# Head, expert stages and their joints rebuilt: routing by token, norms on ScalarE, a new order of weight pieces

## What is computed

```python
x = x + ssm(layernorm(x))          # diagonal complex state space, 64 states, then W_out and b_out
x = x + experts(layernorm(x))      # 8 experts, each token takes its 2 best by router logits
x = x + attention(layernorm(x))    # 16 heads of 64, softmax(q k^T + relative bias) v, Wo
x = x + experts(layernorm(x))      # the same expert weights again

# experts(x): g = sigmoid(two largest logits), divided by their sum
for e in range(8):
    ge = sum(g where the token's choice is e)
    out += ge[:, None] * ((silu(x @ w_gate[e]) * (x @ w_up[e])) @ w_down[e])
```

## Time and profile before

| | us |
|---|---|
| median of 3 runs | 902.26 (902.04 to 903.08) |
| profiled execution | 905.03 |
| its span | 903.2 |
| head, to the first expert product | 0 to 74.31 |
| first pass of expert stage 0 (eight steps) | 74.31 to 129.21 |
| other steps of stage 0 | 129.21 to 229.97 |
| between them and the first scores | 229.97 to 244.87 |
| attention's slots | 244.87 to 723.27 |
| its end and the first pass of stage 1 | 723.27 to 791.29 |

### The profile page before, as it was taken

How to read it: one execution, slowest core, us unless ns; L and a number is a source line. 1 busy time by engine, 2 the same in 40 slices (tenths; PEclk the granted TensorE clock), 3 DMA queues, 4 the chain that set the end, 5 groups by cost and what they waited for, 6 DMA issues and landing times.

```text
span 903.2 us, 13948 instructions
## 1 busy us (share of the span) xinstructions
PE 819.9 (91%) x4320; PEld 547.8 (61%) x4320; DVE 658.6 (73%) x1664; ACT 515.1 (57%) x1121; POOL 442.9 (49%) x464
## 2 busy tenths in 40 slices
PE   1867699999779999999999999999999996899997
PEld 0555478888545556556556565565565564688875
DVE  7998477787788776767776767767777646687876
ACT  2214365665466766666566665657656644556664
POOL 3350389998234333433333333334333423789994
PEclk9698899999999999999999999999999997999999
DMA  7001345438300000000000000000000012436621
GB/s 210 3 1 30 85 74 85 90 84 241 122 1 1 1 1 1 1 1 1 1 1 1 1 2 1 1 1 1 1 1 1 1 37 72 96 80 84 79 70 47
DMA packets 53265, 36.40 MB, mean 40 GB/s; under 512 B 2209, under 2 KB 50721, under 8 KB 53201
## 3 DMA queue, kind: packets, MB, share of 16 engines
q1 hardware_dynamic: 53200, 35.61, 17.7%
HBM read 34.35 MB, written 1.25 MB: 39 GB/s over the span
## 4 chain that ended last, share of the span: by engine, by line
PE 75%; DVE 11%; issue 4%; POOL 3%; DMA 3%; ACT 2%; SPq 0%; POOLq 0%; DVEq 0%; ACTq 0%
PE bank L839 13%; PE bank L822 12%; PE bank L809 11%; PE bank L222 10%; PE bank L411 9%; PE bank L224 8%; PE bank L223 8%; PE bank L775 3%; POOL hid_lo L688 3%; DMA gates<-gatesT 1%; DVE x_norm L263 1%; DMA gate_all<-gates 1%; DVE ln_stats L237 1%; DVE prob L884 1%; PE bank L277 1%
## 5 line engine op out<-in xcount | busy, mean ns | idle before, releaser
L1028 POOL TENSOR_SCALAR prob<-prob,inv_total 128x512 f32<-128x512 f32 x256 | 175.1, 697 | 317.3 <-DVE inv_total L873 317.3
L688 POOL TENSOR_TENSOR hid_lo<-hid,hid_hi 128x512 fp32r<-128x512 f32 x128 | 192.1, 1518 | 92.3 <-ACT hid_hi L476 90.4
L977 ACT ACTIVATE prob<-prob,peak 128x512 f32<-128x512 f32 x256 | 185.8, 726 | 47.5 <-DVE peak L884 47.5
L884 DVE CUSTOM_DVE_ANT_0 prob<-bank,bias_band 128x512 f32<-128x512 f32 x256 | 166.6, 689 | 31.0 <-PE bank L809 25.1
L822 PE MATMUL bank<-ident,prob 128*128 128x128 f32 x1024 | 136.5, 277 | 3.1 <-ACT probT L983 1.8
L839 PE MATMUL bank<-probT,v 128*64 128x512 f32 x512 | 138.2, 620 | 0.8 <-ACT oT L988 0.8
L559 DVE TENSOR_TENSOR hid<-hid,gate_all 128x512 f32<-128x512 f32 x128 | 123.6, 970 | 19.0 <-DMA gate_all<-gates 15.2
L822 PEld LDWEIGHTS bank<-ident,prob 128*128 128x128 f32 x1024 | 119.8, 143 | 23.9 <-issue 7.2
L550 DVE TENSOR_TENSOR hid<-silu,bank 128x512 f32<-128x512 f32 x128 | 87.0, 684 | 57.8 <-PE bank L224 39.7
L476 ACT CAST hid_hi<-hid 128x512 fp32r<-128x512 f32 x128 | 78.8, 618 | 61.2 <-DVE hid L559 58.1
L466 ACT ACTIVATE silu<-bank 128x512 f32<-128x512 f32 x128 | 76.1, 599 | 61.8 <-PE bank L224 57.5
(11 more groups left out here) (171 smaller groups left out, 1266.1 us busy)
## 6 DMA issues: line engine op xcount, KB each, us to landing
gate_all<-gates SPq DMA_DIRECT2D x12, 1024.0 KB, 15.5
bias_band<-bias_rows SPq DMA_DIRECT2D x16, 448.0 KB, 11.5
gate_all<-gates SPq DMA_DIRECT2D x16, 256.0 KB, 4.9
w_raw<-in_w_gate SPq DMA_DIRECT2D x16, 128.0 KB, 14.5
w_raw<-in_w_up SPq DMA_DIRECT2D x16, 128.0 KB, 10.5
w_raw<-in_w_down SPq DMA_DIRECT2D x16, 128.0 KB, 8.7
x_res<-in_x SPq DMA_DIRECT2D x4, 256.0 KB, 4.7
out<-x_res SPq DMA_DIRECT2D x4, 256.0 KB, 2.3
```

Source lines behind the costliest of these rows:

```text
L688: nc.gpsimd.tensor_tensor(hid_lo[:, buf, m, :], hid[:, buf, m, :], hid_hi[:, buf, m, :].bitcast(F32), ALU.subtract).then_inc(q["hl"], 1)
L884: nc.vector.tensor_tensor_reduce(out=prob[:, buf, h, :], in0=bank[2 * (n % 2) + h][:, :], in1=row_bias, scale=-1.0, scalar=NEG_START, op0= ...
L977: nc.scalar.activation(prob[:, buf, h, :], prob[:, buf, h, :], ACT.Exp, bias=peak[:, buf, h:h + 1], scale=-1.0, accum_out=total[:, buf, h: ...
L1028: nc.gpsimd.tensor_scalar(prob[:, buf, h, :], prob[:, buf, h, :], inv[:, buf, h:h + 1], 1.0, ALU.mult, ALU.mult).then_inc(a_n, 1)
```

## The change

- **Head.** The state layer's products are plain float32, one where there were three. The angle operations, seven and not eight, come before the norm of rows. The root has 11 links. Where the norm is applied by ScalarE (ln_apply: layer 0, the first expert stage, chunk 0 of attention's, chunk 3 of the second expert stage's), VectorE makes a shift for it. Other copies go to ScalarE. Weights of experts 0 and 1 are split in the head, and for stage 1 in attention's last batch.
- **Routing** is token-wise: 128 tokens are the stationary operand, the router's 16 columns (hi and lo of 8 experts) move, and VectorE adds hi and lo (route_sum). It goes in parts, chunks 0, 1 and 2, 3 in stage 0; chunks 0 to 2 within attention's slots and chunk 3 after them in stage 1. The gates of expert 0 are spread by TensorE into PSUM (route_spread; all chunks in stage 0, chunk 3 in stage 1), the others by DMAs of 256 KB.
- **Order.** First and last pass go by chunk (BY_CHUNK: both experts on chunks 0 and 1, then both on 2 and 3), the middle ones by expert. All are written out. hid has four buffers in the first pass.
- **Weight pieces** are placed by tables: position in the pass, then (par, passes ahead, piece). Two semaphores, `wu` after the up piece and `wd` after the down piece, take the place of `w`.
- **Ends.** The sums of chunks 0 and 1 are turned within the last steps, and in stage 0 the norm statistics of chunk 0 are made there. The last downs and attention's first projections are interleaved, and so are attention's end and the first steps of stage 1.

```diff
+            ln_link(dve, k, nc.vector.tensor_scalar(rstd[:, tiles].bitcast(U32), var[:, tiles].bitcast(U32), -0.5,
                                                     RSQRT_START, ALU.mult, ALU.add))
...
+        def ln_shift(dve, k, c0, c1):
+
+            tiles = slice(c0 * QT, c1 * QT)
+            nc.vector.scalar_tensor_tensor(out=shift[:, tiles], in0=mv[:, tiles, 0], scalar=-1.0, in1=rstd[:, tiles],
+                                           op0=ALU.mult, op1=ALU.mult).then_inc(LN[k]["rs"], 1)
...
+        def ln_apply(act, k, c, group):
+
+            act.wait_ge(LN[k]["rs"], group + 1)
+            for n in range(c * QT, (c + 1) * QT):
+                last = nc.scalar.activation(xn[:, n, :], x[:, n, :], ACT.Identity, bias=shift[:, n:n + 1],
+                                            scale=rstd[:, n:n + 1])
+            last.then_inc(LN[k]["xn"], 1)
...
-        MOE_LAG = 2
+        LAG = 2
+        BY_CHUNK = [(0, 0), (0, 1), (1, 0), (1, 1), (0, 2), (0, 3), (1, 2), (1, 3)]
+        BY_EXPERT = [(0, 0), (0, 1), (0, 2), (0, 3), (1, 0), (1, 1), (1, 2), (1, 3)]
+        ENDS = (BY_CHUNK, BY_CHUNK)
+        INTO_MIDDLE = (BY_EXPERT, BY_CHUNK)
+        MIDDLE = (BY_EXPERT, BY_EXPERT)
+        INTO_LAST = (BY_CHUNK, BY_EXPERT)
...
+        ROUTED = [[(0, 2), (2, 4)], [(0, 3), (3, 4)]]
+        TURN_BANK = [[5, 7], [7, 7]]
+        IN_PSUM = [(0, 1, 2, 3), (3,)]
...
+        FIRST_PIECES = {6: [(0, 1, 0)], 7: [(0, 1, 1)]}
+        MIDDLE_PIECES = {0: [(0, 0, 2)], 1: [(1, 0, 0)], 2: [(1, 0, 1)], 3: [(1, 0, 2)], 6: [(0, 1, 0)],
+                         7: [(0, 1, 1)]}
+        LAST_PIECES = {0: [(0, 0, 2), (1, 0, 0)], 1: [(1, 0, 1)], 2: [(1, 0, 2)]}
+
+        def first_of(order, pos):
+            return order[pos][0] not in [par for par, _ in order[:pos]]
+
...
+            for j in range(QT):
+                tok = slice((c * QT + j) * P, (c * QT + j + 1) * P)
+                dst, both = bank[home][:, j * 2 * E:(j + 1) * 2 * E], rw[:, :, :].rearrange("p r e -> p (r e)")
+                nc.tensor.matmul(dst, xh[:, tok], both, start=True, stop=False)
+                last = nc.tensor.matmul(dst, xl[:, tok], both, start=False, stop=True)
...
+        def route_spread(pe, k, c):
...
+            for j in range(QT):
+                n = c * QT + j
+                last = nc.tensor.transpose(bank[4 + c][:, j * P:(j + 1) * P],
+                                           MEM[k]["gates"][:, n, 0:1].to_broadcast([P, P]), ident[:, :])
+            last.then_inc(q["gb"], 1)
...
+        def gate_up(pe, k, i, order, pos, half, first=False):
+
+            q, m = MOE[k], MEM[k]
+            s, (par_, c) = 8 * i + pos, order[pos]
+            tok = slice(c * BANK, (c + 1) * BANK)
+            if half == 0 and first_of(order, pos):
+                pe.wait_ge(q["wu"], 2 * i + par_ + 1)
...
+        def experts_tensor(pe, k, rest):
+
+            for i in range(1, HALF - 1):
+                for pos in range(8):
+                    expert_step(pe, k, i, INTO_MIDDLE if i == 1 else MIDDLE, pos)
+            for pos in range(8):
+                gate_up(pe, k, HALF - 1, BY_CHUNK, pos, 0)
+                down(pe, k, HALF - 1, INTO_LAST, pos)
+                if pos == 7:
+                    sums_turn(pe, k, 1)
+                gate_up(pe, k, HALF - 1, BY_CHUNK, pos, 1)
+                if pos == 5:
+                    sums_turn(pe, k, 0)
+            rest(lambda: down(pe, k, HALF, ENDS, 0), lambda: down(pe, k, HALF, ENDS, 1))
...
+            lo, hi = PIECES[piece]
+            act.wait_ge(q["ld0"] if par_ == 0 else q["ld1"], 48 * (i + ahead) + 48)
+            if not first:
+                if piece == 2:
+                    act.wait_ge(q["d"], 8 * (i + ahead) - (2 if par_ == 0 else 0))
+                elif par_ == 0:
...
+        def pool_step(pool, k, i, pos, pieces, deep=2, first=False):
+            s = 8 * i + pos
+            low_of(pool, k, s, pos, 0, deep, first and pos < 2)
+            for par_, ahead, piece in pieces.get(pos, ()):
+                weight_low(pool, k, 2 * (i + ahead) + par_, par_, piece)
+            low_of(pool, k, s, pos, 1, deep, first and pos < 2)
+
...
+            def routing(n):
+                if n == MAX_AT:
+                    route_max(dve, 1, 0)
+                if INDEX_AT <= n < INDEX_AT + 2:
+                    c0, c1 = ((0, 1), (1, 3))[n - INDEX_AT]
+                    route_index(dve, 1, 0, c0, c1)
+                if n == WEIGH_AT:
+                    route_weights(dve, 1, 0)
+                if n == PICK_AT:
+                    route_pick(dve, 1, 0)
...
-                pe.wait_ge(LN[0]["lo"], b + 1)
+                pe.wait_ge(LN[0]["hi"], b + 1)
                 if b >= 2:
                     pe.wait_ge(m_z, 4 * (b - 1))
                 for r in range(2):
-                    last = three(pe, bank[2 * (b % 2) + r][:, :], bTh[:, r, :], bTl[:, r, :], xh[:, tok], xl[:, tok])
+                    last = nc.tensor.matmul(bank[2 * (b % 2) + r][:, :], bT[:, r, :], xf[:, tok],
+                                            start=True, stop=True)
...
+            step = lambda pos: expert_step(pe, 0, 0, ENDS, pos, True)
+            both = lambda pos: [gate_up(pe, 0, 0, BY_CHUNK, pos, half, True) for half in range(2)]
+            ln_turn(pe, 1, 0, 4)
+            ln_turn(pe, 1, 1, 5)
+            route_logits(pe, 0, 0, 4)
+            both(0)
+            route_logits(pe, 0, 1, 5)
+            both(1)
+            ln_turn(pe, 1, 2, 6)
+            ln_turn(pe, 1, 3, 7)
+            both(2)
+            route_spread(pe, 0, 0)
+            route_turn(pe, 0, 0)
+            both(3)
+            route_logits(pe, 0, 2, 6)
+            route_logits(pe, 0, 3, 7)
+            route_spread(pe, 0, 1)
+            gate_up(pe, 0, 0, BY_CHUNK, 4, 0, True)
+            down(pe, 0, 0, ENDS, 2, True)
+            gate_up(pe, 0, 0, BY_CHUNK, 4, 1, True)
+            gate_up(pe, 0, 0, BY_CHUNK, 5, 0, True)
+            down(pe, 0, 0, ENDS, 3, True)
+            gate_up(pe, 0, 0, BY_CHUNK, 5, 1, True)
+            route_spread(pe, 0, 2)
+            route_turn(pe, 0, 1)
+            route_spread(pe, 0, 3)
+            down(pe, 0, 0, ENDS, 4, True)
+            gate_up(pe, 0, 0, BY_CHUNK, 6, 0, True)
+            down(pe, 0, 0, ENDS, 5, True)
+            gate_up(pe, 0, 0, BY_CHUNK, 6, 1, True)
+            gate_up(pe, 0, 0, BY_CHUNK, 7, 0, True)
+            down(pe, 0, 0, ENDS, 6, True)
+            down(pe, 0, 0, ENDS, 7, True)
+            gate_up(pe, 0, 0, BY_CHUNK, 7, 1, True)
...
+            experts_tensor(pe, 0, enter)
+            steady()
+            leave()
+            experts_tensor(pe, 1, finish)
...
+            ln_apply(act, 0, 0, 0)
...
-            link(nc.vector.tensor_scalar(ang, ang, 2 * math.pi, PI_BELOW, ALU.mult, ALU.min))
-            nc.vector.tensor_scalar(ang, ang, -PI_BELOW, None, ALU.max).then_inc(s_rot, 1)
...
+            nc.vector.tensor_scalar(ang, ang, HALF_TURN, -HALF_TURN, ALU.min, ALU.max).then_inc(s_rot, 1)
+            for pair in range(2):
+                for c in (2 * pair, 2 * pair + 1):
+                    dve.wait_ge(x_in[c], 16)
+                ln_rows(dve, 0, 2 * pair, 2 * pair + 2)
...
```

More of the change, by code:

```diff
@@ L371, in route, with route_pick @@
+        def route_pick(dve, k, part):
+            m, (c0, c1) = MEM[k], ROUTED[k][part]
+            tiles, sl = (c1 - c0) * QT, slice(c0 * QT, c1 * QT)
+            pick = [m["pick"][:, r, sl] for r in range(2)]
             iota_all = iota8[:, :].unsqueeze(1).to_broadcast([P, tiles, E])
             for r in range(2):
[L373 removed]
+                last = nc.vector.tensor_tensor(pick[r], iota_all, m["topf"][:, sl, r:r + 1].to_broadcast([P, tiles, E]),
@@ new lines, in product, with products @@
+        def product(dve, k, s, pos, half, deep=2, first=False):
+            q, m = MOE[k], MEM[k]
+            dve.wait_ge(q["sg"], 2 * s + half + 1)
+            dve.wait_ge(q["u"], 2 * s + half + 1)
+            if not first:
+                dve.wait_ge(q["hl"], 2 * s + half + 1 - 2 * deep)
+            nc.vector.tensor_tensor(m["hid"][:, pos % deep, half, :], m["silu"][:, half, :], bank[2 * half + 1][:, :],
+                                    ALU.mult).then_inc(q["mul"], 1)
+        def products(dve, k, s, pos, deep=2, first=False):
+            for half in range(MT):
+                product(dve, k, s, pos, half, deep, first)
```

1351 lines of the change are left out of this document (742 added, 609 removed).

## The result

| | before | changed |
|---|---|---|
| median of 4 runs | 902.67 us | 931.28 us (930.04 to 934.97) |
| ratio | | 1.032 (95% interval 1.029 to 1.036) |
| profiled execution, its span | 905.03, 903.2 | 934.97, 933.2 |

What follows compares the result with a forecast made beforehand. TensorE was taken to bound the kernel, busy 91% of the span and nearly full in steady expert steps. Terms -15.8 - 1.4 + 13.8 + 1.4 + 4.2 - 3.0 + 13.8 = +13.0 gave 915.3 us, range 886 to 926.

Steps and rivals of the forecast that it cites:

- a: Head: first states at about 22.9, first expert product at 58.5; -15.8 us (bounds -9 and -20).
- b: First pass of stage 0, now by chunk: old gate waits go, new waits come; -1.4 us (bounds -8 and +4).
- c: Later expert passes: TensorE pauses for w_lo at three places per stage, low clock behind; +13.8 us in each stage.
- d: From the last down group into attention's first scores: sums, turns and norm roots moved; +1.4 us.
- e: Attention: routing of three chunks in its last batch's slots, 3.2 us on TensorE and 1.0 for VectorE; +4.2 us.
- f: Out of attention and through the first pass of stage 1: 65 us against 68.02; -3.0 us (bounds -10 and +3).
- rival 2: Ragged ends come near TensorE's own work and attention absorbs its routing, pauses stay: 898 us; chance 0.20.
- Rival 1: No pauses in the expert passes, since w_lo comes before it is wanted: 887.7 us; chance 0.08.
- Rival 3: Head gains under 9 us and low clock covers more of first passes and pauses: 925 us; chance 0.14.

Runs made afterwards that it cites:

- e4_pool: e2_all, with GpSimd's w_lo of expert 1 and second qk_lo in the head held until after VectorE's norm ahead of the experts: 889.25 us, repeated 890.27.
- e1_middle: Changed kernel with the next pair's up piece made at position 6 instead of 7 in first and middle passes: 903.66 us, ratio to before 0.997.
- e2_all: e1_middle, with the second expert's up piece in the last pass made at position 0 (down piece at 1): 892.10 us, ratio 0.985.
- e3_late: Kernel before, with the next expert's three weight pieces made at chunks 1, 2 and 3 instead of 0, 1 and 2: 975.38 us, ratio 1.078.
- e6_route: e4_pool, with VectorE's routing of chunk 3 at the begin of stage 1 ahead of step 4's products: 880.80 us, repeated 884.18.

## Why the prediction was wrong, step by step

In spans (the profiled execution's forecast of 918.0 less the 1.8 around its span), forecast 916.2, measured 933.2: 17.0 us missing. The mechanism of the largest term, the pauses, was right. The steps that failed are sizes: the low clock behind pauses (3.6 us stood for it in each stage, 7.1 and 6.5 came, and 3.9 more than forecast in the first pass), and the head, where VectorE's norm beside GpSimd was taken at its undisturbed length (10.0 us, 13.7 came). Attention came out 6.0 us under its forecast and hid part of this; without it 23.0 us would be missing. By stretch, change against before:

| stretch | forecast | measured | in e4_pool |
|---|---|---|---|
| a, head | -15.8 | -9.9 | -15.2 |
| b, first pass, stage 0 | -1.4 | +2.9 | -1.3 |
| c and d, to the first scores | +15.2 | +20.6 | +1.9 |
| e, attention | +4.2 | -1.8 | +1.5 |
| f, first pass, stage 1 | -3.0 | -0.1 | -3.9 |
| c, rest of stage 1 and tail | +13.8 | +18.3 | +1.9 |

**c, the mechanism: right.** The waits were forecast at 3.2, 3.2 and 3.8 us in each stage; they are 3.36, 3.36, 3.59 and 3.36, 3.36, 3.60. e1_middle and e2_all take them away, e3_late puts them into the kernel before. The idle VectorE did make the last w_lo quick (0.72), but the two hid_lo ahead of it stood beside VectorE's gate products (L624) and took 3.51 us together, so the pause was not 2.8. Of what part c worked out from the Trainium skill, the quick last piece is so in this trace and the shorter pause is not.

**c, the clock: mis-sized, the first of the failing steps.** I took "two in three of such stretches, 1.2 each" and counted three pauses in each stage. The stretch from the ninth step on also holds the low clock behind the pause at its own start, so there are four, and each costs 1.1 to 2.3 us: steps of 6.33, 5.63, 6.82 and 5.84 in stage 0, where the same steps without a pause last 4.25, 4.50, 4.50 (e1_middle) and 4.28 (e4_pool). That is 7.1 us where 3.6 stood, and 6.5 in stage 1. The rows it came from show an attention whose TensorE was half busy ahead of the low clock; here a TensorE that was wholly idle for 3.4 us worked up to 5.6 us at the lower level. A row with a whole stop was at hand in the kernel before, in its first pass:

```profile
92.20:95.70 3.50, 0.00 (x0) 0.00 (x0) 1.29 (x2) 0.89 (x2) 0.77 (x2) 1.00 0.20 60
95.70:102.50 6.80, 4.67 (x14) 3.78 (x15) 4.92 (x28) 3.56 (x7) 2.99 (x3) 0.50 0.24 73
```

This is the stop of 6.41 us of the earlier trace rows. It goes on to 97.83, so the clock fell while TensorE still stood, and 4.67 us of work ran at 0.50: 2.3 us of cost. The stop is nearly twice as long as the pauses of part c, so the row gives their upper end and not their mean.

**b, the first pass of stage 0: the clock again.** I put the pause at its end at "about 3, partly the same time". It was 5.95 us, since the step ahead of it was itself held up; the clock behind it falls into c. The other waits were shorter in turn: TensorE is idle 13.67 of 57.80 us, and 13.5 stood in the sum. But it is busy 44.13 and not 40. By the trace's clock it works 13.7 of these at the lower level, which is 6.9 us of cost where 3 stood; the work left, 37.3 at full clock, is the 37 forecast. e1_middle, without the pause, has 53.1 for b. That this is close to the forecast of 53.5 is luck, since the forecast held the pause.

**a, the head: the norm's chain was priced without GpSimd beside it.** The first states began at 22.3, forecast 22.9 (the terms listed add up to 22.6). Up to the norm it went 2.3 us slower than forecast (50.8 and not 48.5), but e2_all, with the same code there, begins it at 48.4: this varies. From there 13.7 us and not 10.0, and e4_pool shows why: GpSimd's work on weights, which the change moves into the head, lies beside VectorE's norm. The prediction named the Trainium skill's rule on VectorE and GpSimd and applied it only to the pauses, where it favoured the change; whether it also held in the chain of 11 links beside the new work of GpSimd I did not ask. The kernel before had a hint, at the same place in its head. A link that takes 0.17 us as the median of ten took 1.94, and it ended at 61.49, with GpSimd's qk_lo at 61.46:

```profile
56.79 4.67 POOL L1235 TENSOR_TENSOR qk_lo<-qk_f,qk_hi 128x1024 fp32r<-128x1024 f32 x2
59.55 1.94 DVE L248 TENSOR_SCALAR ln_var<-ln_mean_var 128x12 f32<-128x12 f32 x1
```

**d and the steps beside the pauses.** From the end of the last gate product to the first scores it is 15.63 us and not 14.90: +0.7, forecast +1.4. In it a wait of 3.3 us for the norm is followed by a low clock too (0.60 in 246.90:250.30). I forecast nothing beside pauses and clock for the rest of either stage, and in e4_pool, where the pauses are gone, it is +2.2 and +1.9: steps in which two weight pieces are made, sums are turned, or the last wait of 0.7 us stands last 4.4 to 5.0 us and not 4.2.

**e, attention: wrong sign, and the clock is why.** The routing in its slots was to cost 4.2 us. The stretch is 476.64 against 478.40, and between 476.6 and 481.5 in the builds above, which have the same attention. What varies is mostly TensorE's clock, as e6_route and its repeat show (columns as in the earlier trace rows):

```profile
232.59:709.21 476.62, 464.10 (x2797) 274.82 (x2797) 348.89 (x1020) 313.23 (x756) 177.32 (x260) 1.00 0.02 5
232.05:713.50 481.45, 470.11 (x2796) 278.38 (x2796) 349.15 (x1020) 313.47 (x756) 177.88 (x260) 0.99 0.02 5
```

By the traces' clock TensorE works no time at the lower level in the first and 13.7 us in the second, at a cost of 6.8: its busy time is 6.0 us longer for the same products. The stretch is 4.8 us longer, and the two whole executions differ by 4.2. In the kernel before it is 9.9 us and in the changed one 3.4, so 3.2 us of the change are clock, which no term had. With it taken out, TensorE's work grew by 2.8 us (forecast 3.2) and its idle time shrank by 1.3 (forecast +1.0): +1.5 and not +4.2. VectorE took its part in its idle time, which rival 2 had said. Of the 6.0 us by which attention beat its forecast, 3.2 are thus luck.

**f.** The waits of TensorE are 2.99, 2.98 and 5.95 us, forecast 2.0, 2.8 and 6, and 3.26 at the boundary, forecast 3.3. Of the missing 2.9 us, 1.5 are waits (15.6 in all, 14.1 forecast) and 1.3 TensorE's busy time. In that the clock was short again (5.8 us of cost, 1 stood for it), and the work was put too high (46.5 us at full clock, 50 stood).

**Rival 1 and 2.** Without the pauses the time would have been 887.7 by rival 1; e4_pool, which has no pauses but one of 0.7 us in each stage, is at 889.25, and e2_all, which lacks the edit in the head, at 892.10. So the sum of all other terms was right to 2 to 4 us, though single terms were off by up to 6 in both directions: in part luck. The gains that rival 2 lists add up to more than the 17 us it took off; it didn't come, so nothing hangs on this. Rival 3 (low clock over more of the stretches, 925) had the right direction for what failed (a short head, and more low clock), and was held too small.

## What to carry to other kernels

Where an engine is full and another prepares its operands, compare, piece by piece, the time from the start of the step in which a piece is made to its being ready with the length of that step: here 7.5 us against 4.18, so a piece made in the last step before its use costs a pause, however idle its maker is on average. A short whole stop of TensorE costs about half as much again in clock (1.7 us for 3.4 here, on average). And when work moves to GpSimd, look for the chain of short VectorE instructions that will run beside it, and when a wait names an engine, look first at what stands ahead of the awaited instruction in its queue: one swap of order there gave 6.6 to 7.6 us. Where builds differ by a few us, compare how long TensorE's clock was low in a stretch that the edit doesn't touch, before the edit gets the credit.
